# Adding gathered expert rows into the residual by the DMA, on one Trainium2 core

## The reference, cut to what matters

```
x = x + 0.5 * expert_ffn(norm(x))     # stage 0: 4 experts, each token to one
x = x + attention0(norm(x))           # stage 1: 16 heads, linear in the sequence length
x = x + 0.5 * expert_ffn(norm(x))     # stage 2: as stage 0
x = x + 0.5 * sparse_ffn(norm(x))     # stage 3: 32 experts, the best 4
x = x + attention1(norm(x))           # stage 4: softmax attention with rotation
x = x + 0.5 * sparse_ffn(norm(x))     # stage 5: as stage 3
```

## Time and profile before

| | us |
|---|---|
| median of 3 runs | 2547.51 |
| lowest, highest | 2541.93, 2551.03 |
| the profiled execution's own time | 2552.19 |
| its span | 2550.4 |
| stage 0's matmuls | 116 to 262 of the span |
| stage 1 | 262 to 545 |
| stage 2's matmuls | 545 to 706 |

### The profile page before, as it was taken

How to read it: one execution, slowest core, us unless ns; L and a number is a source line. 1 busy time by engine, 2 the same in 40 slices (tenths; PEclk the granted TensorE clock), 3 DMA queues, 4 the chain that set the end, 5 groups by cost and what they waited for, 6 DMA issues and landing times.

```text
span 2550.4 us, 39117 instructions
## 1 busy us (share of the span) xinstructions
PE 2252.5 (88%) x11234; PEld 1572.7 (62%) x11234; DVE 1999.4 (78%) x4669; ACT 1298.6 (51%) x1907; POOL 962.2 (38%) x868
## 2 busy tenths in 40 slices
PE   4399476749949999986999999999999998999999
PEld 3377355537737777764555555555555555777777
DVE  6588577748848999975888888888888885888887
ACT  1088232218824444442666666666666665444444
POOL 6600566420047777762122111112111202565654
PEclk9999655659969999996999999999999999999999
DMA  7243111024348888871111211111111113889886
GB/s 176 74 155 128 42 31 35 22 95 133 112 104 182 172 186 171 185 166 51 59 59 63 69 62 55 61 55 58 58 54 59 54 54 84 181 174 187 174 186 152
DMA packets 141318, 266.47 MB, mean 104 GB/s; under 512 B 19347, under 2 KB 22422, under 8 KB 140950
## 3 DMA queue, kind: packets, MB, share of 16 engines
q1 hardware_dynamic: 132790, 247.99, 39.7%
q0 software_dynamic: 8416, 17.25, 2.6%
HBM read 213.26 MB, written 54.31 MB: 105 GB/s over the span
## 4 chain that ended last, share of the span: by engine, by line
PE 59%; issue 12%; DVE 11%; DMA 7%; ACT 6%; SPq 3%; POOL 1%; POOLq 0%; DVEq 0%; ACTq 0%
PE ps L1960 10%; PE ps L1984 9%; PE ps L1971 8%; PE ps L1679 7%; PE ps L1681 7%; PE ps L1680 7%; DMA gate_rows<-gates_dram 4%; DVE m L1369 2%; ACT g L854 2%; PE ps L1693 1%; ACT g_hi L827 1%; PE ps L1686 1%; PE ps L1706 1%; DVE g_lo L1051 1%; DVE xnT_hl L1051 1%
## 5 line engine op out<-in xcount | busy, mean ns | idle before, releaser
L1533 DVE TENSOR_REDUCE shift<-ps 128x1 fp32r<-128x512 f32 x1024 | 664.2, 685 | 157.7 <-PE ps L1960 139.7
L978 ACT ACTIVATE prob<-ps 128x1024 f32<-128x1024 f32 x512 | 509.8, 1025 | 361.7 <-PE ps L1971 354.9
L827 ACT ACTIVATE hi<-m 128x512 fp32r<-128x512 f32 x512 | 318.8, 631 | 424.0 <-DVE m L1369 423.9
L679 POOL TENSOR_TENSOR lo<-m,hi 128x512 fp32r<-128x512 f32 x256 | 342.5, 1340 | 306.2 <-ACT hi L827 305.7
L1960 PE MATMUL ps<-k_pad,q_st 128*128 128x512 f32 x1024 | 401.7, 434 | 19.7 <-DVE shift L1533 12.9
L1369 DVE SCALAR_TENSOR_TENSOR m<-ps,gate_rows 128x512 f32<-128x512 f32 x512 | 335.0, 680 | 90.8 <-PE ps L1681 51.9
L1960 PEld LDWEIGHTS ps<-k_pad,q_st 128*128 128x128 f32 x1024 | 179.4, 190 | 263.7 <-DVE shift L1533 229.7
L1971 PE MATMUL ps<-q_sh,k_pad 128*128 128x512 f32 x1024 | 329.8, 404 | 0.0
L1984 PE MATMUL ps<-prob,v_cols 128*32 128x512 f32 x2048 | 272.7, 605 | 1.2 <-ACT o_raw L827 0.8
L1051 DVE TENSOR_TENSOR lo<-m,hi 128x512 fp32r<-128x512 f32 x256 | 209.8, 819 | 16.7 <-ACT hi L827 0.2
L1679 PE MATMUL ps<-hi,vals_hl 128*128 128x512 f32 x512 | 209.9, 410 | 0.7 <-DVE lo L1051 0.5
(11 more groups left out here) (215 smaller groups left out, 3997.1 us busy)
## 6 DMA issues: line engine op xcount, KB each, us to landing
gate_rows<-gates_dram SPq DMA_DIRECT2D x256, 512.0 KB, 6.4
w_blk<-w_dram SPq DMA_DIRECT2D x38, 514.5 KB, 3.6
q_st<-q_dram SPq DMA_DIRECT2D x64, 256.0 KB, 2.6
k_pad<-k_dram SPq DMA_DIRECT2D x256, 50.0 KB
k_dram<-qk_hl SPq DMA_DIRECT2D x48, 256.0 KB
q_dram<-qk_hl SPq DMA_DIRECT2D x48, 256.0 KB
x_blk<-sorted_x SPq DMA_DIRECT2D x38, 256.0 KB, 3.4
sorted_y<-yb_rows SPq DMA_DIRECT2D x38, 256.0 KB, 2.0
```

The costliest lines, as they stand in the source:

```text
L679: pool.tensor_tensor(m["lo"][:, s], m["m32"][:, s], m["hi"][:, s].bitcast(F32), ALU.subtract).then_inc(sig(ph, "lo_pool"), 1)
L827: return act.activation(o, i, ACT.Copy)
L978: act.activation(prob[:, h % HP, 2 * half:2 * half + 2, :], ps[:, b0:b0 + 2, :], ACT.Exp, scale=SCALE).then_inc(sig(ph, "prob"), 1)
L1533: dve.tensor_reduce(shift[:, g % 2, b, c:c + 1], wide(PASS1 + b % 2), AXX, ALU.max, negate=True).then_inc(sig(ph, "qmax"), 1)
```

## The change

Stage 0's rows no longer go through a buffer. The indirect DMA of `collect(0, t)` adds the rows into `x` in SBUF itself (`compute_op=ALU.add`). The factor 0.5 moves to the copy of the expert's result out of PSUM, which becomes a multiplication by a scalar in stage 0 (it stays a copy in stage 2). `add_back(0, t)` is gone from stage 1, and the buffers `y_back_a` with it. `moments(1, t)` waits for the gathers' semaphore, and `collect(0, n)` waits for the statistics of tile n-2 in place of its addition. Stage 2's rows still go through a buffer and VectorE.

```diff
-        y_back_a = [early_sb(f"y_back_a{b}", [P, BLK, D]) for b in range(2)]
...
-                if t >= 2:
-                    pool.wait_ge(sig(ph, "x_done"), 4 * (FIRST[ph] + t - 1))
+                if t >= 2 and ph == 0:
+                    pool.wait_ge(sig(1, "stats"), t - 1)
+                elif t >= 2:
+                    pool.wait_ge(sig(ph, "x_done"), 4 * (t - 1))
                 for b in range(BLK):
                     c = t * BLK + b
-                    pool.indirect_dma_start(
-                        y_back[ph][t % 2][:, b, :], None, sorted_y,
-                        bass.IndirectOffsetOnAxis(ap=y_row[:, c:c + 1], axis=0)).then_inc(back[t % 2], 16)
+                    rows = bass.IndirectOffsetOnAxis(ap=y_row[:, c:c + 1], axis=0)
+                    if ph == 0:
+                        pool.indirect_dma_start(x[:, c, :], None, sorted_y, rows,
+                                                compute_op=ALU.add).then_inc(back[t % 2], 16)
+                    else:
+                        pool.indirect_dma_start(y_back[t % 2][:, b, :], None, sorted_y,
+                                                rows).then_inc(back[t % 2], 16)
...
-                pass_wait(dve, sig(ph - 1, "x_done"), (t - FIRST[ph] + FIRST[ph - 1]) * 4 + 4)
+                pass_wait(dve, sig(ph - 1, "x_done"), (t - FIRST[ph]) * 4 + 4)
...
-                if ph > 0:
-                    dve.wait_ge(sig(ph - 1, "x_done"), 4 * t + 4)
+                if ph == 1:
+                    dve.wait_ge(back[t % 2], 64 * (t // 2 + 1))
+                elif ph == 2:
+                    dve.wait_ge(sig(1, "x_done"), 4 * t + 4)
...
-                    copy(yb_rows[n % 2][:], rows4(YB)).then_inc(sig(ph, "yb_rows"), 1)
+                    if ph == 0:
+                        dve.tensor_scalar(yb_rows[n % 2][:], rows4(YB), 0.5, None, ALU.mult)\
+                           .then_inc(sig(ph, "yb_rows"), 1)
+                    else:
+                        copy(yb_rows[n % 2][:], rows4(YB)).then_inc(sig(ph, "yb_rows"), 1)
...
-                    if here(5):
-                        add_back(0, t + 5)
```

More of the change, by code:

```diff
@@ L277, in macaron @@
         ffn1_mem = dict(ffn1_memory(), **routing)
-        y_back = {0: y_back_a, 2: ffn1_mem["y_back"]}
+        y_back = ffn1_mem["y_back"]
         gates_dram = nc.dram_tensor("gates_dram", (2, E1, SEQ), F32).ap()
@@ L692, in collect_on @@
                     pool.indirect_dma_start(
-                        y_back[2][q][:, b, :], None, sorted_y,
+                        y_back[q][:, b, :], None, sorted_y,
                         bass.IndirectOffsetOnAxis(ap=y_idx[:, q, b:b + 1], axis=0)).then_inc(back[q], 16)
@@ L1185, in add_back @@
                 xt = x[:, t * BLK:t * BLK + BLK, :]
-                dve.scalar_tensor_tensor(out=xt, in0=y_back[ph][t % 2][:], scalar=0.5, in1=xt, op0=ALU.mult,
+                dve.scalar_tensor_tensor(out=xt, in0=y_back[t % 2][:], scalar=0.5, in1=xt, op0=ALU.mult,
                                          op1=ALU.add).then_inc(sig(ph, "x_done"), 4)
@@ L1380, in step @@
                         dve.wait_ge(back[p], (t - p) * 32 + 64 * (TILES // 2 + 2))
-                        dve.scalar_tensor_tensor(out=x_tile(ph, t + 2), in0=y_back[2][p][:], scalar=0.5,
+                        dve.scalar_tensor_tensor(out=x_tile(ph, t + 2), in0=y_back[p][:], scalar=0.5,
                                                  in1=x_tile(ph, t + 2), op0=ALU.mult, op1=ALU.add)\
```

## The result

Over 13 runs of each, in alternation, the changed kernel takes 2539.54 us in the median (2534.04 to 2543.94) against 2548.19 (2541.93 to 2551.92): a ratio of 0.9966, 95% interval 0.9957 to 0.9975, 8.65 us less. The forecast was 2538.9. The number is right, and most of its terms are not: the start became slower, not faster, and as much time as the whole gain comes from stage 4, whose code the change does not touch.

A forecast was written before the change was run, and what follows sets the result against it. Stage 1 was taken as bound by a loop through several engines, with POOL setting the pace at its beginning. -7.4 (loop) - 2.4 (start) + 1.2 (issue) = -8.6 us, from 2547.51 to 2538.9 us, range 2535 to 2545.

The forecast's parts named there:

- The sum: Whole kernel: -7.4 us in stage 1's loop, -2.4 in its start, +1.2 for gather issue, together -8.6 us.
- the price of the adding gather: POOL's issue in stage 1: the add puts 0 to 0.46 us on each gather, taken as 0.1, thus +1.2 us.
- The prediction's own sign of failure: Stage 1's gathers: the prediction fails if their group's duration is 1.5 us or above; 1.0 to 1.1 was expected.
- Rival (a): Stage 1's start: adding gathers' issue eats the gain, start loses 6 to 14 us, total around 2547; chance 0.22.
- D: POOL in stage 1: extra time the add puts on issuing one gather, counted twelvefold at the start; taken as 0.1 us.
- The order of POOL's work: Stage 1's later rounds: gathers come after the moments, `root(1)` waits some 5.1 us behind them; costed at nothing.
- The point named: Stage 1's later rounds: four adding gathers must add over about 2.5 us (14.7 - 12.2), 0.6 each, to count.
- The start's mechanism: Stage 1's start: `apply_norm` of tile 0 no longer waits behind tile 2's addition and starts 2.4 us earlier.
- The landing: Stage 1's gathers: a longer landing than some 2.6 us is covered, by 2.7 us at tile 0; costed at nothing.
- The loop: Stage 1, rounds 0 to 10: without the addition each is 0.67 us shorter from logits to `outT`, 7.4 us.
- rival (c): Stage 1's rounds: TensorE, waiting less, holds the better clock; gain grows to 13 us or more, 2534; chance 0.08.
- The half: Stage 0: 19 of 38 PSUM copies `yb_rows` become multiplications of the same 684 ns; costed at nothing, at most 0.4 us.

The follow-up runs named there:

- e3: The kernel before with only the factor 0.5 moved to the copy from PSUM, addition factor 1: 2548.94 us, ratio to before 1.0002.
- e8: The kernel before with 96 idle instructions (tiny memsets) on VectorE at the end of stage 1: 2538.14 us, ratio to before 0.9959.
- e7: The changed kernel with 32 idle instructions (tiny memsets) on VectorE at the end of stage 1: 2549.61 us, ratio to before 1.0002.
- e12: The changed kernel with 64 idle instructions (tiny memsets) on VectorE at the end of stage 1: 2546.11 us, ratio to before 0.9997.
- e1: The changed kernel with plain gathers that overwrite `x`, so the first layer's residual sum is left out: 2518.40 us, ratio to before 0.9892.
- e4: The changed kernel with `root(1, t+4)` put before `collect(0, t+6)` on GpSimd: 2533.58 us, ratio to before 0.9945.
- e11: The changed kernel with every tile through a buffer and VectorE addition, no adding gather, root first, 105 idle instructions: 2528.95 us, ratio to before 0.9933.
- e9: The changed kernel with tiles 0 to 4 through a buffer and VectorE addition, root first, 110 idle instructions: 2532.34 us, ratio to before 0.9934.
- e2: The kernel before, order and VectorE addition kept, with first-layer gathers adding into the buffer: 2556.70 us, ratio to before 1.0039.

## Why the prediction was right, and where it was wrong

**The sum.** Forecast, by the table's columns: -1.9 in the start (-2.4 + 1.2, and -0.7 for the addition of round 0), -6.7 in the rounds. In the two profiled executions: start +5.6, rounds -9.2, `outT` 10 to 15 -0.4, stage 4 -9.2, the rest +0.4 (what stands between), together -12.8, the difference of the spans. The medians differ by less, 8.65. Errors of +7.4 (start), -2.5 (rounds) and -9.2 (stage 4) cancelled for the greater part. The -9.2 of the rounds is itself partly chance. Three profiled kernels have before's rounds (before, e3, e8: 149.2, 147.0, 144.3) and three the changed kernel's (after, e7, e12: 140.0, 142.4, 141.9): the means differ by 5.4, less than forecast, and start and rounds together come to 192.2 and 192.4. At the same place of the code the change gives nothing (e7, e12), and before at a good place is as fast as the change (e8). The forecast has to be called right by luck. Its range had a slip too: -4.3 with 3 us of clock ends at 2546, not 2545.

**The step that failed: the price of the adding gather.** "From above by the rows 0.46" was no bound: the slowest plain gather says nothing of an operation that the trace does not have. It is 0.59. "I take 0.1, near the median" made +1.2 of what is 7.1 for the twelve alone. The prediction's own sign of failure, the gathers' group at 1.5 us or above, came true: 1.556. Rival (a), D between 0.5 and 1.2 and an end near 2547, is what the edit itself did. The estimate from the Trainium skill ("DMA: Bandwidth & Descriptors", section "SWDGE vs HWDGE vs iDMA"), D of about 0.5, was nearer than the 0.1. That an add needs a second read descriptor, on which it rests, no run here shows.

**The order of POOL's work, costed at nothing.** The point named, D above 0.6, was just about reached: the ten take 14.8 us and not 12.2 + 4 x 0.59 = 14.6, and six later rounds wait for `root(2)`, 0.16 us once and 1.43 to 1.50 us five times, between 387 and 462. The round to set against it was also not 14.7: rounds 4 to 6 of the changed kernel, ahead of these waits, take 13.4 to 13.5 us, so by estimate a D above 0.3 ((13.4 - 12.2) / 4) was enough.

**The start's mechanism was right,** -2.4 without the add, and -0.7 for the addition of round 0: e1 measured -3.1. The landing is covered, as said, as long as `root` comes last (e4): from the fourth gather's start to the reader 3.44 us (278.76 - 275.32) against 2.62, of which 0.6 is the issue.

**The loop.** 0.67 us a round from the logits to `outT` was right: rounds 2 to 10 take 4.24 to 4.37 us there after, 4.91 to 4.92 before. e1 against e11 gives 7.5 us for ten rounds. What the adding gathers then take back is the waits for `root(2)`. That a shorter wait of TensorE shifts the clock was rival (c), at 0.08. It isn't shown: e8, with before's loop, has the 0.66 of after, so the pattern moves by itself from one profiled execution to the next, by 5 us in the rounds. Whether the change shifts it besides stays open.

**The half** cost nothing (e3).

**Not foreseen at all: the place of code.** That the edit leaves other stages alone was never written down, only assumed. The change took 32 instructions out of VectorE's program (2891 to 2859), 16 additions and 16 waits. Stage 4's loop of 336 moved from 2177 to 2145, and no longer stops 2.3 us for instructions in each of six passes: 14.0 us of stops, 9.2 of the stage. That the place does it is shown both ways, by e7 and by e8. The repetition at 128 was a guess, and e8 to e11 agree with it. Packets are 8.2 KB (0.61 MB / 74), and the Trainium skill ("Perfetto Trace Analysis", section "The 4-stage abstract model") says that instructions are of 64 bytes, by which 128 of them are 8192 bytes. That the loop must lie in three pieces of 128 and not four fits all fourteen kernels, but so does that it must lie in two pieces of 256 and not three, and no run tells them apart. Before with 128 idle instructions (place 2305) would: by the first it stops, by the second not. Where the lower edge of the good places is was not tried either.

Stage 3, which nothing touched, took 519.2 to 522.5 us in these executions, without a pattern by edit. That is left open.

## What to carry to other kernels

Compare unchanged stages of both traces before you credit an edit with its gain: here a stage 900 us on, moved by 32 instructions, gave all of it. Where a loop's rows show a stop with "issue" once per pass and the instruction queue keeps fetching, pad the code ahead of it by a few dozen idle instructions and look again; here that is worth more than any other single edit that keeps the result (11 us against e4's 6). Profile a kernel more than once before a part of a stretch is put down to an edit: with the same rounds these took 144.3 to 149.2 us. For an operation that the trace does not have, rows of its plain form are a lower bound, not an upper one. The adding gather was paid at its issue, above all where twelve stood in a row ahead of a small instruction that others waited for; with the order of the two put right, the version without any adding gather was no slower (e11 against e9).

## What the runs showed of the hardware

- An indirect gather of 128 rows of 512 bytes that adds takes GpSimd 1.556 us, a plain one 0.958 (0.976 into `x` itself, e1). Whether it adds into `x` or into a buffer makes no difference (e2: 1.567).
- The software queue moved 15584 packets for 17.25 MB after, 8416 for the same bytes before. The 7168 more are 112 for each of the 64 gathers.
- A VectorE loop of 336 instructions, 117 us a pass, loses 2.3 to 2.7 us in each of six passes at some places of the code and none at others; the instruction queue moves 74 packets over the whole kernel where it stops, and 44 or 45 where it does not.
- Copy and multiplication by a scalar from PSUM, 128x512, fp32: 683 and 684 ns.
